# Self-attention pass of a two-layer decoder: four projections computed as three single-pass products of split operands

## The reference

```python
B, S, C = x.shape
H, Dh = (N_HEAD, HEAD_DIM)                      # 16 heads of 16
qkv = (x @ w_qkv).reshape(B, S, 3, H, Dh)
qkv = jnp.transpose(qkv, (2, 0, 3, 1, 4))
q, k, v = (qkv[0], qkv[1], qkv[2])
q = _layernorm(q, q_gamma, q_beta)
k = _layernorm(k, k_gamma, k_beta)
logits = jnp.einsum('bhsd,bhtd->bhst', q, k) / (math.sqrt(Dh) * T)
att = jax.nn.softmax(logits, axis=-1)
out = jnp.einsum('bhst,bhtd->bhsd', att, v)
out = jnp.transpose(out, (0, 2, 1, 3)).reshape(B, S, C)
return out @ w_proj
```

## Time and profile before

| what | value |
|---|---|
| time, median of 3 runs | 2739.05 us (2736.01 to 2741.09) |
| span of the profiled execution | 2732.5 us |
| the profiled execution's own time | not listed; the median of the runs is 6.55 us over its span |
| PE busy | 2354.2 us (86%) |
| DVE busy | 1869.3 us (68%) |
| ACT busy | 1643.3 us (60%) |
| POOL busy | 1352.9 us (50%) |
| mean granted clock of PE | 0.941 |

### The profile page before, as it was taken

One profiled execution on the slowest core, in us unless ns is written; L12 is line 12 of the kernel. 1 busy time (PEld: TensorE's weight loads), 2 busy tenths in 40 slices (PEclk: granted clock), 3 DMA queues, 4 the chain that ended last, 5 costly groups with the idle time before them and its releaser, 6 DMA issues. The chain is left out here.

```text
span 2732.5 us, 49486 instructions
## 1 busy us (share of the span) xinstructions
PE 2354.2 (86%) x16048; PEld 1842.8 (67%) x16048; DVE 1869.3 (68%) x4490; ACT 1643.3 (60%) x3283; POOL 1352.9 (50%) x1313
## 2 busy tenths in 40 slices
PE   5999999669999958999999999986999898599881
PEld 3667676559999835565665656654787777599881
DVE  3888888545656437777777777772777777477783
ACT  3777777545555426776766767663444343388883
POOL 4777777453334255455454545521556565202556
PEclk9999999779999978999999999996999999799996
DMA  2222222152222001111111111113233433355896
GB/s 62 73 67 74 70 71 66 40 168 73 86 65 66 18 29 32 42 39 43 41 41 42 38 42 39 33 39 127 86 117 121 137 124 107 128 160 181 275 279 199
DMA packets 236524, 241.65 MB, mean 88 GB/s; under 512 B 36926, under 2 KB 222528, under 8 KB 236144
## 3 DMA queue, kind: packets, MB, share of 16 engines
q1 hardware_dynamic: 214704, 192.11, 23.0%
q0 software_dynamic: 20480, 46.39, 5.3%
q10 hardware_dynamic: 1088, 0.00, 0.0%
HBM read 132.78 MB, written 101.25 MB: 86 GB/s over the span
## 5 line engine op out<-in xcount | busy, mean ns | idle before, releaser
L1554 DVE TENSOR_REDUCE f_nm<-f_raw 128x4 f32<-128x1024 f32 x256 | 312.8, 1222 | 107.5 <-PE f_raw L1667 104.6
L1390 POOL TENSOR_TENSOR f_hm<-f_hm,f_mhalf 128x64 f32<-128x64 f32 x32 | 366.4, 11449 | 2.7
L1459 ACT ACTIVATE f_PT<-f_sco 128x1024 f32<-128x1024 f32 x256 | 262.2, 1024 | 99.1 <-PE f_sco L1684 98.7
L2399 POOL DMA_INDIRECT d_pick<-expert_out,e_out_slots x128 | 133.2, 1041 | 221.7 <-DMA expert_out<-d_eo 135.7
L916 ACT ACTIVATE b_hT<-b_H,b_b1r 128x512 f32<-128x512 f32 x128 | 88.4, 691 | 162.4 <-PE b_H L1046 147.0
L1684 PE MATMUL f_sco<-f_q4T,f_k4T 64*128 64x256 f32 x1024 | 130.9, 336 | 51.0 <-DMA f_q4T<-f_nmT 36.6
L1925 POOL DMA_INDIRECT expert_in<-g_xm,e_slots x128 | 129.8, 1014 | 40.2 <-issue 37.0
L677 PE MATMUL a_bank<-a_w,a_xnT 128*128 128x512 f32 x256 | 127.1, 621 | 21.9 <-ACT a_xnT L394 21.9
L1061 PE MATMUL b_O<-b_w2l,b_hTh 128*128 128x256 f32 x512 | 145.9, 285 | 0.0
L1061 PE MATMUL b_O<-b_w2h,b_hTh 128*128 128x256 f32 x512 | 144.7, 283 | 0.0
L1061 PE MATMUL b_O<-b_w2h,b_hTl 128*128 128x256 f32 x512 | 143.6, 280 | 0.0
(11 more groups left out here) (368 smaller groups left out, 7722.3 us busy)
## 6 DMA issues: line engine op xcount, KB each, us to landing
e_xs<-expert_in SPq DMA_DIRECT2D x85, 256.0 KB, 3.3
expert_out<-d_eo SPq DMA_DIRECT2D x85, 256.0 KB, 2.5
x_scratch<-a_x SPq DMA_DIRECT2D x64, 256.0 KB, 3.1
b_w<-in_L_ffn_W_dram SPq DMA_DIRECT2D x16, 1024.0 KB, 5.7
a_x<-in_x_dram SPq DMA_DIRECT2D x32, 256.0 KB, 3.8
a_cx<-in_ctx_dram SPq DMA_DIRECT2D x32, 256.0 KB, 3.4
f_x<-x_scratch SPq DMA_DIRECT2D x32, 256.0 KB, 2.7
f_q4T<-f_nmT SPq DMA_DIRECT2D x128, 64.0 KB, 2.3
```

Source lines behind the costliest of these rows:

```text
L1390: g.tensor_tensor(hm[b % 2][:, :], hm[b % 2][:, :], mhalf[:, :], ALU.pow).then_inc(hroot, 1)
L1459: s.activation(PT[n % 3][:, t, :, :], heads(SCO), ACT.Exp, scale=float(DH) ** -0.5).then_inc(probs_ready, 1)
L1554: v.tensor_reduce(nm[:, t, g * HG:(g + 1) * HG], heads(RAW), AX.X, ALU.max, negate=True)\
L2399: g.indirect_dma_start(pick[b % GR][:, t, c, :], None, ex.eo_d[k], bass.IndirectOffsetOnAxis(ap=ex.out_slots[:, b, t, c:c + 1], axis=0), b ...
```

## The change

The four projections become products of split operands. ACT's two copies out of PSUM now write the high parts `xh` (from A) and `onh` (from Z). Two new parts of DVE, "in low" and "out low", subtract them from the bank to get the low parts `xl` and `onl`; they, and no longer ACT's copies, mark the bank as taken. In `ORDER` "in low" stands behind "qk gamma" and "out low" behind "raw 3". The weights are split once: ACT writes `wqkvh` and `woh`, DVE writes `wqkvl` and `wol` in the first slot. PE does three matmuls of one pass where it did one product of float32.

```diff
         ORDER = (
             "qk scale", "in stats", "raw 0", "att 0", "raw 1", "out o0", "att 1", "in norm", "out o1", "raw 2",
-            "att 2", "head var", "in normT", "qk gamma", "out oT", "att 3", "raw 3", "in qk0", "in qk1", "out proj",
+            "att 2", "head var", "in normT", "qk gamma", "in low", "out oT", "att 3", "raw 3", "out low", "in qk0", "in qk1", "out proj",
...
+            act.wait_ge(w.prepared, 7)
+            s.activation(wqkvh[:, :, :], wqkv[:, :, :], ACT.Copy).then_inc(w_high, 1)
+            s.activation(woh[:, :, :], wo[:, :, :], ACT.Copy).then_inc(w_high, 1)
+
+            def take_xT_high(b):
                 wait_full(act, "in normT", b)
                 if b:
                     wait_full(act, "in v", b - 1)
-                s.activation(xnT[:, :, :], halves(A), ACT.Copy).then_inc(taken("in normT"), 1)
+                s.activation(xh[:, :, :], halves(A), ACT.Copy).then_inc(xT_high, 1)
...
-                s.activation(onT[:, :, :], halves(Z), ACT.Copy).then_inc(taken("out oT"), 1)
+                s.activation(onh[:, :, :], halves(Z), ACT.Copy).then_inc(onT_high, 1)
...
                 last.then_inc(xn_ready, 1)
                 if b == 0:
+                    split_weights()
                     initial_values()
+
+            def split_weights():
+                dve.wait_ge(w_high, 1)
+                v.tensor_tensor(wqkvl[:, :, :], wqkv[:, :, :], wqkvh[:, :, :].bitcast(F32), ALU.subtract).then_inc(w_split, 1)
+                dve.wait_ge(w_high, 2)
+                v.tensor_tensor(wol[:, :, :], wo[:, :, :], woh[:, :, :].bitcast(F32), ALU.subtract).then_inc(w_split, 1)
+
+            def take_xT_low(b):
+                dve.wait_ge(xT_high, b + 1)
+                v.tensor_tensor(xl[:, :, :], halves(A), xh[:, :, :].bitcast(F32), ALU.subtract).then_inc(taken("in normT"), 1)
+
+            def take_onT_low(b):
+                dve.wait_ge(onT_high, b + 1)
+                v.tensor_tensor(onl[:, :, :], halves(Z), onh[:, :, :].bitcast(F32), ALU.subtract).then_inc(taken("out oT"), 1)
...
-            def project(bank, srcT, weight):
-                for t in range(T):
-                    for c in range(C):
-                        last = t_.matmul(halves(bank)[:, t, :], srcT[:, c, t * P:(t + 1) * P], weight[:, c, :],
-                                         start=c == 0, stop=c == C - 1)
+            def split_products(out, t, pairs):
+                for c in range(C):
+                    for n, (x, w_) in enumerate(pairs):
+                        last = t_.matmul(out, x[:, c, t * P:(t + 1) * P], w_[:, c, :],
+                                         start=c == 0 and n == 0, stop=c == C - 1 and n == 2)
                 return last
+
+            def of_qkv(cols):
+                high, low = wqkvh[:, :, cols], wqkvl[:, :, cols]
+                return (xh, low), (xl, high), (xh, high)
...
-                for c in range(C):
-                    last = t_.matmul(bank[:, :], xnT[:, c, t * P:(t + 1) * P], wqkv[:, c, 0:2 * D],
-                                     start=c == 0, stop=c == C - 1)
-                last.then_inc(full(f"in qk{t}"), 1)
+                if b == 0:
+                    pe.wait_ge(w_split, 1)
+                split_products(bank[:, :], t, of_qkv(slice(0, 2 * D))).then_inc(full(f"in qk{t}"), 1)
...
-                project(Z, xnT, wqkv[:, :, 2 * D:3 * D]).then_inc(full("in v"), 1)
+                for t in range(T):
+                    last = split_products(halves(Z)[:, t, :], t, of_qkv(slice(2 * D, 3 * D)))
+                last.then_inc(full("in v"), 1)
...
-                project(A, onT, wo).then_inc(full("out proj"), 1)
+                if b == 0:
+                    pe.wait_ge(w_split, 2)
+                for t in range(T):
+                    last = split_products(halves(A)[:, t, :], t, ((onh, wol), (onl, woh), (onh, woh)))
+                last.then_inc(full("out proj"), 1)
```

More of the change, by code:

```diff
@@ L1232, in attention_pass @@
         wqkv, wo, gam, bet = w.wqkv, w.wo, w.gam, w.bet
+        wqkvh, wqkvl = sb("wqkvh", [P, C, 3 * D], F32R), sb("wqkvl", [P, C, 3 * D], F32R)
+        woh, wol = sb("woh", [P, C, D], F32R), sb("wol", [P, C, D], F32R)
         x, xr = sbn("x", 2, [P, T, D]), sbn("xr", 2, [P, T, D])
         st, mv, rs = sb("st", [P, T, 6]), sb("mv", [P, T, 2]), sb("rs", [P, T])
-        xn, xnT = sb("xn", [P, T, D]), sb("xnT", [P, C, S])
+        xn = sb("xn", [P, T, D])
+        xh, xl = sb("xh", [P, C, S], F32R), sb("xl", [P, C, S], F32R)
         sq = sb("sq", [P, T, 2 * H, DH])
@@ L1245, in attention_pass @@
         rden = sb("rden", [P, T, H])
-        on, onT = sb("on", [P, T, D]), sb("onT", [P, C, S])
+        on = sb("on", [P, T, D])
+        onh, onl = sb("onh", [P, C, S], F32R), sb("onl", [P, C, S], F32R)
         consts, dve_consts = sem("consts"), sem("dve_consts")
@@ L1253, in attention_pass @@
         squared = sem("squared")
+        w_high, w_split, xT_high, onT_high = sem("w_high"), sem("w_split"), sem("xT_high"), sem("onT_high")
         hvar, hstep, hroot, scaled, qk_ready = sem("hvar"), sem("hstep"), sem("hroot"), sem("scaled"), sem("qk_ready")
@@ L1396, in _ @@
             s = nc.scalar
-            def take_xnT(b):
+            act.wait_ge(w.prepared, 7)
+            s.activation(wqkvh[:, :, :], wqkv[:, :, :], ACT.Copy).then_inc(w_high, 1)
+            s.activation(woh[:, :, :], wo[:, :, :], ACT.Copy).then_inc(w_high, 1)
+            def take_xT_high(b):
                 wait_full(act, "in normT", b)
@@ L1473, in take_onT @@
                     wait_full(act, "out proj", b - 1)
-                s.activation(onT[:, :, :], halves(Z), ACT.Copy).then_inc(taken("out oT"), 1)
+                s.activation(onh[:, :, :], halves(Z), ACT.Copy).then_inc(onT_high, 1)
             slots({
-                "in normT": take_xnT, **numbered("in qk", take_qk, T), "in v": take_v, "qk high": high,
+                "in normT": take_xT_high, **numbered("in qk", take_qk, T), "in v": take_v, "qk high": high,
                 **numbered("qk split", take_split, SRND),
@@ L1581, in _ @@
                 "in stats": stats, "in norm": norm, "head var": head_var, "qk scale": head_scale,
-                "qk gamma": head_gamma, "qk low": low, **numbered("qk split", take_split, SRND),
+                "qk gamma": head_gamma, "in low": take_xT_low, "out low": take_onT_low, "qk low": low, **numbered("qk split", take_split, SRND),
                 **numbered("raw ", raw_max, FR), **numbered("raw shift", shift, T),
```

## The result

The changed kernel takes 2806.23 us (median of 4 runs, 2798.17 to 2809.37), against 2737.66 us for the kernel before in the same comparison. The ratio is 1.0247, with a 95% interval of 1.0221 to 1.0274: slower. The profiled execution has a span of 2805.3 us, 72.8 us above that of before.

A forecast was written before the change was run, and what follows sets the result against it. DVE's queue, not PE, the busiest engine, was taken to set the slot: PE waits for `xl`. Loop 26.5, clock 36.7 and start 5.1 us make 68.3 on the 2732.5 span: 2800.8, plus 6.55: 2807 us, range 2762 to 2856.

The forecast's parts named there:

- The loop: Full slots: DVE sets the pace and PE waits for `xl`; 27.52 us a slot instead of 25.91, 26.5 us lost.
- The bank's second wait: Before "in qk1": PE waits 0.34 us for `onl` to free Z, leaving 1.16 of the 1.50 us saved.
- The clock: After PE's wait at "in qk0": 3.4 us at half speed in each slot, 1.36 us a slot, 36.7 us.
- the sign of a clock near 0.5 in most slots: Expected in the changed kernel's profile: clock near 0.5 in and after "in qk0" of most slots.
- Start: First slot: "in low" stands behind DVE's initial values, delaying "in qk0" by 5.1 us; slots 1 to 3 cost nothing.
- End: After the last projection of queries: "out proj" saves 0.38 us in five slots, `onl` is added; costed at nothing.
- The weight loads: Rival for PE's projections: 36 loads a slot bind, only 0.45 of 1.50 us saved; 2836 us, chance 0.03.
- The last step: From span to median of the runs: the kernel before's 6.55 us added to 2800.8, giving 2807 us.

The follow-up runs named there:

- the filler: Changed kernel plus ten matmuls of 512 columns, results unread, on PE in front of "in qk0" from item 5 on: 2782.8 us, ratio 1.0169.
- the kernel with float32 products: Kernel before plus DVE's two subtractions and their waits where the change puts them, projections still float32, low parts unused: 2849.3 us, ratio 1.0426.

## Why the prediction was right

The forecast was 2807 us and the kernel takes 2806. The steps one by one:

- **The loop.** Forecast 27.52 us a slot at full clock, measured 27.74 in the three undisturbed slots above. The wait in front of "in qk0" was forecast at 2.77 us; the rows have 2.77, 2.80 and 2.84 behind undisturbed slots. The 0.2 us missing are two small terms. `xl` to PE takes 0.83 us and not 0.74: the handover was taken as 0.05 us, which is what PE needed after DVE's copy at 1358.19 in the kernel before (1358.47 to 1358.52), and is 1551.73 - 1551.58 = 0.15 here. And "raw 5" comes 7.99 us after "in qk0", where 9.02 - 1.16 = 7.86 was forecast, because the split matmuls take longer than in the expert phase's stream. PE's timeline of the slot from 1524.00, with the offsets that the text uses:

```profile
1525.63 0.50 PE L1625 MATMUL f_Z<-f_wqkvl,f_xh 128*128 128x512 f32 x1
...
1527.13 0.28 PE L1625 MATMUL f_A<-f_wol,f_onh 128*128 128x256 f32 x1
...
1528.44 0.28 PE L1625 MATMUL f_A<-f_woh,f_onh 128*128 128x256 f32 x1
1528.65 0.50 PE L1696 MATMUL f_raw<-f_k4T,f_q4T 64*128 64x256 f32 x4
...
1530.40 0.36 PE L1625 MATMUL f_Z<-f_wqkvl,f_xh 128*128 128x256 f32 x1
1530.61 0.28 PE L1625 MATMUL f_Z<-f_wqkvh,f_xl 128*128 128x256 f32 x1
...
1531.99 0.50 PE L1696 MATMUL f_raw<-f_k4T,f_q4T 64*128 64x256 f32 x4
```

  "out proj" takes 1.52 us and "in v" 1.59, where 1.44 was taken for each. The extra lies at the ends of a group, 0.21 us where the stream had 0.12. With this the busy time of the projections in such a slot is 6.36 us against 7.48 before, 15% lower and not a fifth.
- **The bank's second wait.** "in qk1" starts 1.63 us after "in qk0", forecast 1.74, and "out proj" 3.13 us after, forecast 3.14. That `onl` is on the path was shown when only `xl` was moved, and the view of its subtraction (L1538) in the changed kernel names who waited for it, us and times:

```profile
  PE f_A L1625: 11.1, 5
  PEld f_Z L1625: 10.2, 24
```

  The 24 are weight loads of "in qk1"; the five are taken up below.
- **The clock.** That the clock falls after the wait was right; how often was not. The forecast had a fall in nearly every slot, 1.36 us each, 36.7 us. The mean slot from "in qk0" of slot 4 to that of slot 31 is 28.56 us, (1835.76 - 1064.61) / 27, against 27.74 undisturbed: 0.82 us a slot, 22 us, and the filler gave back 21. The disturbed slot shown above costs 1.5 us more, near the 1.36 taken, but the trace has the clock at half right after the wait in nine of the 27 slots only (those from 1093.58, 1180.03, 1238.17, 1323.29, 1380.31, 1466.94, 1579.48, 1665.60 and 1750.31); they are 1.3 to 3.2 us longer, 16 us in all. Waits of 2.77 and 2.80 us were followed by none. Three more slots, from 1209.30, 1410.58 and 1608.73, have a fall during the scores alone and are 0.9 to 1.4 us longer, though the prediction let PE's wait cover those. So the sign of a clock near 0.5 in most slots did not come, and what decides whether a wait is followed by a fall stays open. The rows that end at 1835.76 and start at 1064.61:

```profile
1064.61 0.77 PE L1625 MATMUL f_A<-f_wqkvl,f_xh 128*128 128x512 f32 x1 [0.36 <-DVE f_xl L1534]
...
1835.76 0.47 PE L1625 MATMUL f_A<-f_wqkvl,f_xh 128*128 128x512 f32 x1 [2.73 <-DVE f_xl L1534]
```

- **Start.** Up to "in qk0" of slot 4 the start was costed at 5.1 us and cost 1064.61 - 1052.25 = 12.4. The first wait was right: 5.90 us where it was 0.78, 5.12 more.

```profile
983.83 0.77 PE L1625 MATMUL f_A<-f_wqkvl,f_xh 128*128 128x512 f32 x1 [5.90 <-DVE f_xl L1534]
```

  Another 0.8 us had passed before the pass began. From there to "in qk0" of slot 4 it is 80.78 us against 74.30: in this stretch, whose slots 1 to 3 were costed at nothing, 6.5 us were missing. PE waits 1.69, 2.68 and 3.41 us in front of "in qk0" in slots 1 to 3 (0.97, 0.78 and none before), and the granted clock is lower, in the windows view 0.80 before (first row) and 0.71 in the changed kernel (second row); what each of the two costs was not separated.

```profile
977.95:1052.25 74.30, 55.29 (x262) 34.46 (x263) 40.32 (x62) 31.94 (x57) 45.13 (x25) 0.80 0.08 23
983.83:1064.61 80.78, 56.75 (x294) 42.46 (x295) 41.79 (x61) 32.34 (x57) 42.44 (x16) 0.71 0.08 20
```

- **End.** The last slots were costed at nothing. The last residual's addition, in the kernel before and in the changed one:

```profile
1879.86 0.69 DVE L1578 TENSOR_TENSOR f_xr<-f_xr,f_A 128x512 f32<-128x512 f32 x1 [5.80 <-PE f_A L1601]
```

```profile
1956.05 0.69 DVE L1602 TENSOR_TENSOR f_xr<-f_xr,f_A 128x512 f32<-128x512 f32 x1 [3.08 <-PE f_A L1625]
```

  From "in qk0" of slot 31 to it are 110.99 us before and 120.29 after, 9.3 more. "out proj" waits for `onl` there, five times and 11.1 us together (the five of the view above, at 1866.3, 1890.7, 1915.6, 1938.1 and 1953.1). The phases behind the pass, which the change does not touch, took 3.4 us less in this execution: 72.8 - 12.4 - 27 x (28.56 - 26.54) - 9.3.
- **The weight loads** do not bind. The kernel without low parts has all 36 loads a slot and is the fastest of all.

So the closeness of the total is partly luck. On the span the clock's term was 15 us too large, the loop's (6 us), the start's (7 us) and the end's (9 us) were too small, and the other phases gave 3 back: 2800.8 was forecast and 2805.3 measured. The last step was off the other way. The 6.55 us from span to median belonged to one execution of the kernel before and not to the kernel; the median of the changed one is 0.93 us above its span. What was argued from the order of the queues came out best: the length of an undisturbed slot within a hundredth, and the wait in it within 0.1 us.

## What to carry to other kernels

Before work is moved from a busy engine to one with idle time, look at where in its queue the new instruction stands and what the receiver needs at that moment: VectorE was idle for a quarter of the time, but not there, and 0.6 us of work became a wait of 2.8 us. An instruction that now frees a bank takes over every waiter of that bank, so follow the bank's next user too: with only the first subtraction moved the kernel took 2827 us. Place it in the queue where its input has just become ready, ahead of work that nobody waits for yet.

## What the runs showed of the hardware

A wait of about 1 us on TensorE in each slot (1.02 us in the row above), with shorter ones of 0.37, 0.30 and 0.16 us near it, was followed in 12 of 27 slots of the kernel before by a fall of its clock to half (their mean is 26.54 us, an undisturbed one takes 25.91). Four matmuls whose results nobody reads, put into that wait, kept the clock at 1.00 and made that kernel faster by 0.57% (ratio 0.9943). Here idle time on the busiest engine has a second price, which appears after the wait and on other instructions. It is seen in the granted clock of the windows view and in the length of the matmuls behind the wait (3.34 us for 1.96 in the kernel with float32 products). Which waits are followed by a fall is not settled: of the 27 waits in front of "in qk0" in the changed kernel nine were.
